# State-space stage: the output projection of the preceding tile at the front of a slot instead of at its end

## What is computed

```python
proj = hidden_states @ in_proj_w.T                     # gate z, xBC, dt
xBC = silu(causal_conv4(xBC) + conv_b)                 # x, B, C; 8 groups of 16 heads of 64
# per chunk of 128 tokens, per head:
scores = einsum('bclhn,bcshn->bchls', C, B) * Lmat     # Lmat = exp(cs_l - cs_s), lower triangle
Y = scores @ (x * dt)  +  (C * exp(cs)) @ state  +  x * D
yg = y * silu(gate)
rstd = rsqrt(mean(yg**2 over the group of 1024) + EPS)
out = (yg * rstd * norm_w) @ out_proj_w.T              # summed over all 8192 channels
```

## Time and profile before

| | before |
|---|---|
| time, median of 3 runs (lowest, highest) | 2499.95 us (2497.55, 2501.27) |
| the profiled execution's own time | 2498.26 us |
| its span | 2496.5 us |
| TensorE busy | 2385.7 us, 96% of the span |
| VectorE, ScalarE, GpSimd busy | 1780.5, 1588.5, 1227.0 us |
| granted TensorE clock, mean | 0.984 |
| state-space slots: first scan, last of 128 scans | 66.58 us, about 1552 us |

### The profile page before, as it was taken

One profiled execution on the slowest core, in us unless ns is written; L12 is line 12 of the kernel. 1 busy time (PEld: TensorE's weight loads), 2 busy tenths in 40 slices (PEclk: granted clock), 3 DMA queues, 4 the chain that ended last, 5 costly groups with the idle time before them and its releaser, 6 DMA issues. The chain is left out here.

```text
span 2496.5 us, 48866 instructions
## 1 busy us (share of the span) xinstructions
PE 2385.7 (96%) x15424; PEld 1370.9 (55%) x15624; DVE 1780.5 (71%) x3227; ACT 1588.5 (64%) x3317; POOL 1227.0 (49%) x986
## 2 busy tenths in 40 slices
PE   5999999999999999999999998879999999999797
PEld 3555555555555555555555555445555555555343
DVE  4677777777777777777777776577777777788422
ACT  5776776776766776766766775355556566565322
POOL 4456556556556556556556459343434434454223
PEclk8999999999999999999999999989999999999899
DMA  6243343343343343343343341320110110100000
GB/s 238 96 138 111 102 137 111 101 137 112 101 137 111 101 139 109 102 140 108 102 140 108 121 152 52 128 97 1 43 43 1 44 43 5 40 18 1 1 0 34
DMA packets 112867, 218.79 MB, mean 88 GB/s; under 512 B 9440, under 2 KB 42848, under 8 KB 110400
## 3 DMA queue, kind: packets, MB, share of 16 engines
q1 hardware_dynamic: 112576, 215.28, 26.4%
HBM read 212.10 MB, written 3.15 MB: 86 GB/s over the span
## 5 line engine op out<-in xcount | busy, mean ns | idle before, releaser
L255 DVE SCALAR_TENSOR_TENSOR xc<-bank,taps,xc 128x511 f32<-128x511 f32 (+2 forms) x384 | 285.0, 742 | 53.2 <-ACT xc L242 35.9
L908 ACT ACTIVATE E<-wq,cst 128x128 f32<-128x128 f32 x1024 | 311.7, 390 | 0.3 <-PEq L289 0.3
L1192 POOL TENSOR_TENSOR xw<-xt,wdec 128x384 f32<-128x384 f32 x128 | 106.5, 832 | 327.0 <-ACT xc L247 163.9
L1201 POOL TENSOR_TENSOR acc<-acc,sq 128x512 f32<-128x512 f32 x112 | 173.2, 1547 | 189.6 <-ACT sq L920 189.6
L1834 POOL TENSOR_TENSOR qT<-qT,qrot 128x512 f32<-128x512 f32 x64 | 81.3, 1270 | 370.2 <-DVE qrot L1725 370.2
L59 PE MATMUL bank<-xhi,wx 128*128 128x512 f16 x640 | 243.2, 380 | 3.3 <-DVE xcB L255 3.3
L1085 DVE SCALAR_TENSOR_TENSOR u<-xc,D,bank 128x512 f32<-128x512 f32 x128 | 95.7, 747 | 209.1 <-PE bank L737 197.5
L60 PE MATMUL bank<-xlo,wx 128*128 128x512 f16 x640 | 243.1, 380 | 0.0
L61 PE MATMUL bank<-xhi,wx 128*128 128x512 f16 x640 | 243.0, 380 | 0.0
L1024 DVE TENSOR_TENSOR E<-E,cbm 128x1024 f32<-128x1024 f32 x128 | 239.5, 1871 | 0.8
L1187 POOL TENSOR_TENSOR ecs<-ecs,xcC 128x768 f32<-128x768 f32 x128 | 234.1, 1829 | 1.7 <-POOLq L289 1.7
(11 more groups left out here) (239 smaller groups left out, 6296.3 us busy)
## 6 DMA issues: line engine op xcount, KB each, us to landing
wq<-cs_rows SPq DMA_DIRECT2D x128, 512.0 KB, 4.1
ecs<-ecs_rows SPq DMA_DIRECT2D x128, 384.0 KB, 3.6
wx<-in_w_xbc SPq DMA_DIRECT2D x80, 256.0 KB, 2.6
wz<-in_w_z SPq DMA_DIRECT2D x64, 256.0 KB, 2.7
wo<-in_w_o SPq DMA_DIRECT2D x64, 256.0 KB, 4.1
wq<-in_wq SPq DMA_DIRECT2D x8, 1024.0 KB, 5.9
awo<-in_wo SPq DMA_DIRECT2D x8, 1024.0 KB, 5.0
wkv<-in_wkv SPq DMA_DIRECT2D x8, 512.0 KB, 3.9
```

The lines of the kernel that those rows point to most:

```text
L255: self.nc.vector.scalar_tensor_tensor(out=dst[:, d:T], in0=self.k.bank[bank][:, 0:T - d], scalar=self.taps[:, bass.ds(g, 1), b, j, 3 - d:4 ...
L908: ins = nc.scalar.activation(E[t.i % 4][:, h, c], sc.csr[t.i % 2][:, h, c * P:(c + 1) * P], ACT.Relu, scale=-1.0, bias=head(sc.cst, t, c, h))
L1201: nc.gpsimd.tensor_tensor(acc[t.b][:], acc[t.b][:], sq[:], ALU.add).then_inc(acc_done, 1)
```

## The change

`output(s-1)`, with its waits and its 12 matmuls, is issued behind `states` and `sum_squares` and ahead of the x projection, instead of behind `turn_x` and the B or C projection. Nothing else is changed: the other engines' programs are what they were, and TensorE issues the same instructions.

```diff
@@ slot (TensorE)
                     if s.i == 0 and not (isinstance(s.u, int) and s.u == 0):
                         pe.wait_ge(bt_done, s.u + 1)
                         sum_squares(1 - s.b, s.u, s.n)
+                    if tile_at(g, m - 1):
+                        for half in range(2):
+                            output(tile_at(g, m - 1), half)
                     t = tile_at(g, m + 3)
                     if t:
                         free_bank(s)
...
                         sc.project(sc.wx[1], nu.b, ring_bank(s.b, USE_C), sc.xp_ready)
-                    if tile_at(g, m - 1):
-                        for half in range(2):
-                            output(tile_at(g, m - 1), half)
                     if nu and s.i == 5:
                         products_CB(nu)
```

## The result

The changed kernel takes 2662.05 us (median of 4 runs, 2656.45 to 2664.18) against 2500.3 us before: a ratio of 1.0646, 95% interval 1.0629 to 1.0663, or 161.8 us more. The forecast was 2632.5 us, in a range of 2600 to 2668: the sign is right, and the 161.8 us are 29 us more than the 132.6 that were forecast.

A forecast was written before the change was run, and what follows sets the result against it. TensorE bounds the state-space stretch (1476.14 of 1500 us busy). Waits of 7.24 + 1.3 = 8.5 us per regular unit give 119.6; with 5.8 + 9.2 - 2 for first unit, last unit and loop edge, 132.6: 2632.5 us, range 2600 to 2668.

The forecast's parts named there:

- The mechanism: ScalarE's tap, released by the x projection, moves 2.59 us; decays and the gate's silu follow, scans wait: 7.24 us per unit.
- Slots 2 and 4: With a B or C projection, these slots last 13.34 us against 13.11 for the silu chain, so they cost 0.
- Its masking then ends near 8.5 us: VectorE in slots 3 and 5: late B and C taps delay u by about 1.8 us, still under 8.90, costing nothing.
- The states' wait: In slots 0, 2, 4 and 6 TensorE's states wait 0.33 us for GpSimd's decayed x: 1.3 us per unit.
- The clock: Rival: TensorE's clock falls to 0.83 across the changed slots, 240 us more, some 2870 us; 5 in 100.
- the pile-up: Rival: delayed B and C taps on VectorE reach masking and convolution; slots 3 and 5 lose another 1 us each, 2665; 7 in 100.
- the clock at 1.00: Sign that the forecast is right: TensorE's clock stays at 1.00 in the stretch; under 0.97 would show it wrong.
- the 14 us that would have pointed at VectorE: Sign that the forecast is wrong: slots 2 and 4 beyond 14 us, meaning VectorE has become the limit.

The follow-up runs named there:

- Between: Kernel before, with the output projection moved behind the x projection and ahead of the gate projection: 2527.74 us, ratio 1.0119.
- half the dose: Kernel before, with only the first 6 of the 12 output matmuls moved ahead of the x projection: 2533.84 us, ratio 1.0144.
- fill_slot0: Changed kernel, with 9 added matmuls at the end of TensorE's work in every slot 0 but the first: 2634.72 us, ratio 1.0541 against the kernel before.
- pool_sum_last: Changed kernel, with GpSimd's sum of squares behind the weight splits in slots 3 to 6: 2641.1 us, ratio 1.0574 against the kernel before.
- decays_first: Changed kernel, with ScalarE's decays issued ahead of the tap instead of behind it: 2631.15 us, ratio 1.0537 against the kernel before.

## Why the prediction was right, and where it was short

**The mechanism** held at each step. ScalarE's tap moved by the full 2.59 us (in slot 3 from 5.39 to 7.99 us behind the start), silu behind decays behind tap, latency of 0.11 us to the scan: slots 3 and 5 were forecast at 11.68 and measured at 11.69 and 11.68. "Between" and "half the dose" showed that it is this chain, and the late x projection in it.

**Slots 2 and 4.** "The B or C projection, which is still behind the gate projection, hides it: 0" is right within the changed kernel (13.50 is 13.34 and the 0.16 us of the states' wait), but not for the reason given alone. "Its masking then ends near 8.5 us, still under the 8.90 at which it is next needed" was the condition, and where the tap is not late (slots 2 and 4 moved alone) it fails: 0.59 us in slot 4, most of the 9 us which that run loses ahead of the last unit.

**The states' wait** was put at 0.33 us, bounds 0 and 0.66. It was 0.16 us in the first sequence and in slots 0 and 2 of the second (the states moved from 1.68 to 1.84 us behind the scan), which takes 0.17 x 4 x 16 = 11 us off the sum. In slots 4 and 6 of the second, where ylo ran beside GpSimd's split, it was 0.48 and 0.39 us more, in seven units: about 6 us back. The slowed ylo (1.22 us for 0.74) was the term that the prediction did not have.

**The clock** is the step that failed; the sum had no term for it. It was left out on the ground that "after idle times of 2.2 us the clock stayed 1.00 in 72 to 79 us". That was one wait, and its scan starts at 79.16 us, so the row ends before anything behind the wait is seen. Behind the wait the clock was 1.00 as well, but one wait of this length does not tell:

```profile
79.00:85.00 6.00, 5.84 (x50) 3.87 (x51) 3.78 (x8) 2.13 (x5) 3.75 (x4) 1.00 0.43 159
```

The share of 16.87 of 20 us, with which the rival was priced, was one that only slots 0 and 6 of the forecast have (11.56 of 13.93); the stage was to be busy for 92%, and was. The rival had been priced for a clock low throughout, 240 us, with 5 in 100; what came was a part of it: scan and states at the lower level behind the two longest waits, 1.65 us in 15 slots 1 and 1.6 us in 7 slots 7, together about 36 us. With these terms the sum is 132.6 - 11 + 6 + 36 = 164, for the 163.2 by which the slots grew in the profiled executions and 161.8 in the medians. That the measured time lies inside the range is luck: its upper end had been drawn to take in the pile-up, and this term was not in it. Of the signs to look for, "the clock at 1.00" did not come (0.97 over the slots, just at the bound named as wrong), and slot 4 of the second sequence, 13.98, stands just under the 14 us that would have pointed at VectorE.

**The pile-up** on VectorE, the third rival, did not occur in the changed kernel: slots 3 and 5 are at 11.69, but for two slots 5 of the first sequence at 11.9 and 12.0.

Taking the load away altogether made slot 0 1.42 us shorter. The Trainium skill (ScalarE: Activation LUTs, What ACT_TABLE_LOAD costs) gives 2.66 us for a load of about 1.28 and a drain of about 1.38; the trace agrees with the load and shows no such drain. Of the clock, the Trainium skill says in TensorE: Matmul & The Clock Gate, A second HAM failure mode, that small idle times between groups of matmuls can let it swing; the waits of 2.2 to 2.6 us in these runs bear that out, though not each of them, and those of 1.0 to 1.6 us do not.

## What to carry to other kernels

When one engine is busy 98% of the time, moving its work costs nothing on that engine itself and can cost a lot through the engines that wait for its results: write down for each of its results when the consumer's chain ends and how much margin is left, slot by slot, before an order is changed. A delay is free up to the smallest of these margins and, in these slots, cost in full from there; follow every chain that leaves the delayed result, not only the one that ends last now, since shortening one shows the next. And price a new wait on TensorE with what follows it: a wait of 2.2 to 2.5 us cost up to 1.6 us more in the clock, and filling one with nine useless matmuls took 27 us off the kernel.

## What the runs showed of the hardware

- A wait of TensorE of 2.2 us was followed by the lower clock in some cases and not in others within one execution: slot 7 was slow in 7 of 15 units in the changed kernel, 7 of 15 in fill_slot0, 1 of 15 in pool_sum_last. Behind waits of 2.44 to 2.54 us slot 1 was slow in 15 of 15 units in the changed kernel and 12 of 15 in pool_sum_last; but in the changed kernel's slot 1 of the first unit (2.38 us) and slots 3 and 5 of the last (2.45 us) the clock was not lowered. The same held for waits ahead of the states in decays_first: 3 of 8 between 2.2 and 2.7 us. Behind waits of 1.0 to 1.6 us, over 200 in these traces, no scan was slow. What decides between two equal waits stays open; a slow scan cost about 1.6 us.
- ScalarE carried out the table load ahead of the wait of the activation that needs it: in "between" the load began at 934.39 and the silu waited until 936.29. The load was hidden in that wait.
- VectorE's 128x512 ylo took 1.22 us beside GpSimd's split and 0.74 us without it; with the sum of squares behind the splits on GpSimd, the overlap was gone and the states' wait behind it fell from 0.78 to 0.30 us.
